# FFN transposes by DMA instead of TensorE, with a new order of work on VectorE and ScalarE

## The chip, the cores and the metric

The kernel runs on one core of a Trainium2 chip. A core has TensorE (PE, with its weight loads PEld), VectorE (DVE), ScalarE (ACT), GpSimd (POOL) and SyncE (SP), which issues DMAs. Each works through its own list of instructions in order; semaphores tie them together. The metric is the time of one execution on the device, in microseconds, lower is better; several runs are summed up by their median.

## The reference

2048 tokens of 512 channels pass through one layer: a linear cross attention, then a gated FFN with quantised weights and activations. The change touches the second part:

```
def activation_quant(x):
    scale = 127.0 / clip(max(abs(x), axis=-1), EPS)
    return clip(round(x * scale), -128, 127) / scale

x   = x + attention(layernorm(x), ctx, ctx, mask, ...)
h   = layernorm(x)
gate = bit_linear(h, w_gate)                # weights -1, 0, 1 times one scale
up   = bit_linear(h, w_up)
a    = up * square(relu(gate))              # 2048 wide
a    = a * rsqrt(mean(square(a)) + 1e-6) * subln_weight
out  = x + bit_linear(a, w_down)            # back to 512 wide
```

`bit_linear` quantises its input by `activation_quant`. So the scale of a row of `a` is known only when all 2048 columns and their squares are there.

## The kernel before

The tokens are 16 tiles of 128 (`NT`). Attention runs first, in four groups of four tiles; beside it the FFN weights are brought to -1, 0, 1 (`tern`, bf16) and the normalised x of groups 0 to 2 is quantised to int8 (`xq`). The last group is quantised within the FFN (`ln2.statistics`, `largest`, `scale`, `quantise`; `cubes` prepares the factors of the scales).

The FFN (`ffn`) is a pipeline over tiles; step s works on tile s with its gate and up products, and on the tiles before it with the rest. For one tile:

- POOL casts `xq` to bf16 `xqb` (L1030, L1033). PE turns it in four 128x128 transposes into PSUM (`turn_x`, L1218), ACT copies it to `xqT` (L1062).
- In four quarters of 512 columns PE computes gate and up (`gate_up`, L1232, 8 products a quarter, two pairs of PSUM banks), ACT takes relu (L1074) and its square, relu2 (L1078), DVE multiplies by up (`multiply`, L1142, writes `acts`), and POOL multiplies by the subln weight (L1048, writes `actg`). ACT sums squares of each half (`squares`, L1085), DVE takes the largest of each half (`largest`, L1147).
- DVE works out the scale in a chain of small operations, `mean` (L1189) to `qs` (L1205), with a square root on ACT (L1108) in it. In the next step it writes the quantised tile `aq` as int16 in one pass (L1156).
- PE turns `aq` in sixteen transposes (L1260) as raw 16-bit patterns, ACT copies them to bf16 `aqT`, changing int16 to bf16 on the way (L1104). A step later PE runs the sixteen down products (L1246), DVE scales them and adds x (`res`, L1167), and SP stores the result (L1016).

The order on each engine is written out by hand. On DVE a step is: multiply 0; aq of the tile before; multiply 1; res of the tile two before; work for the last group of the second layernorm in steps 0 to 7; multiply 2; largest 0; multiply 3; mean, var; largest 1; the rest of the scale. On ACT: quarters 0, 1, 2; copy of xqT; squares 0; quarter 3; squares 1; copies of aqT; square root. On PE: gate_up 0 and 1; down; gate_up 2; turn x; turn aq; gate_up 3. Every engine uses a loop over pairs of steps for the middle of the run. A line `eng.wait_ge(sem, n)` holds the engine until the semaphore has reached n; what follows on that engine waits too.

## Time and profile before

| | us |
|---|---|
| median of 3 runs | 479.37 (477.47 to 481.32) |
| the profiled execution | 475.91 |
| its span from first to last instruction | 474.1 |

The attention takes the first 268 us of the span, the FFN the rest. Busy shares of the page count an engine's instructions; a matmul's end is modelled, so records of PE overlap their successors. "idle before <- releaser" says how long the engine stood before an instruction and what ended that. The page's second part gives the granted clock of PE: full in nearly all of the span, and lower near the end, where PE has little to do.

### The profile page before, as it was taken

Reading aid. Unit: us, or ns where it says so; the run is one execution under the profiler, and the core shown is the slowest. Engines: PE = TensorE matmul, PEld = TensorE weight load, DVE = VectorE, ACT = ScalarE, POOL = GpSimd, SP = SyncE. Lnnn points to the kernel's source line nnn. Section 1 sums busy time; section 2 is a strip of 40 time slices with the busy share of each in tenths; the row PEclk is TensorE's granted clock in tenths of the full one; section 3 lists DMA queues with packets and bytes.
Section 4 is the critical chain, followed back from the end, with each engine's and each line's share of the span. In section 5 each row is a group of like instructions: output and inputs, shape, how many; then the busy total and the mean of one; then the engine's idle time right before and its main releaser. Section 6 shows DMA issues by size and latency. Waiting matters only on the chain. (4 is left out here: it accounts for less than half of the span.)

```text
span 474.1 us, 9209 instructions
## 1 busy us (share of the span) xinstructions
PE 428.0 (90%) x3118; PEld 229.7 (48%) x3136; DVE 382.1 (81%) x869; ACT 338.0 (71%) x538; POOL 155.4 (33%) x145
## 2 busy tenths in 40 slices
PE   4888899997999998999948779999889999999976
PEld 1355546564455653557526334444444444444433
DVE  3588687699989989999898678888888777777772
ACT  5388997494677657775776577777667887888871
POOL 2009200073004600022000145555555555555440
PEclk9998999999899999999987999999999999999999
DMA  7899892004023311232114300000000000000001
GB/s 217 302 395 399 321 365 83 1 2 150 29 91 135 130 47 44 88 99 78 47 45 135 131 1 1 24 22 24 22 25 24 22 24 23 22 22 22 23 24 44
DMA packets 17009, 43.89 MB, mean 93 GB/s; under 512 B 3216, under 2 KB 3216, under 8 KB 16848
## 3 DMA queue, kind: packets, MB, share of 16 engines
q1 hardware_dynamic: 16080, 40.06, 23.7%
q0 software_dynamic: 896, 3.41, 2.0%
q8 instruction: 19, 0.31, 0.3%
q14 instruction: 14, 0.11, 0.1%
HBM read 39.27 MB, written 4.19 MB: 92 GB/s over the span
## 5 line engine op out<-in xcount | busy, mean ns | idle before, releaser
L1048 POOL TENSOR_TENSOR actg<-acts,subln 128x512 f32<-128x512 f32 x64 | 94.7, 1492 | 87.5 <-DVE acts L1142 87.5
L1232 PE MATMUL ps<-tern,xqT 128*128 128x512 bf16 x495 | 113.1, 379 | 4.7 <-DVE acts L1142 1.9
L1232 PEld LDWEIGHTS ps<-tern,xqT 128*128 128x128 bf16 x512 | 48.9, 98 | 61.3 <-DVE acts L1142 4.3
L1246 PE MATMUL ps<-tern,aqT 128*128 128x512 bf16 x255 | 59.2, 385 | 9.5 <-ACT aqT L1104 9.3
L1074 ACT ACTIVATE relu<-ps 128x512 f32<-128x512 f32 x64 | 37.9, 592 | 21.8 <-PE ps L1232 20.9
L1142 DVE TENSOR_TENSOR acts<-relu,ps 128x512 f32<-128x512 f32 x64 | 43.6, 682 | 7.9 <-ACT relu L1078 6.2
L1085 ACT ACTIVATE square<-acts 128x1024 bf16<-128x1024 f32 x32 | 33.7, 1052 | 19.1 <-DVE acts L1142 19.1
L1246 PEld LDWEIGHTS ps<-tern,aqT 128*128 128x128 bf16 x256 | 24.1, 99 | 44.0 <-issue 12.4
L1078 ACT ACTIVATE relu<-relu 128x512 f32<-128x512 f32 x64 | 40.3, 630 | 2.7 <-DVE acts L1142 0.7
L1147 DVE TENSOR_REDUCE amax<-actg 128x1 f32<-128x1024 f32 x32 | 38.8, 1212 | 4.2 <-POOL actg L1048 4.2
L524 DVE SCALAR_TENSOR_TENSOR fl<-ps,fh 128x512 f16<-128x512 f32 x64 | 39.6, 679 | 2.5 <-ACT fh L387 2.5
L387 ACT ACTIVATE qkTh<-ps,bqk 128x512 f16<-128x512 f32 x32 | 21.6, 684 | 21.5 <-PE ps L726 20.6
L387 ACT ACTIVATE fh<-ps 128x512 f16<-128x512 f32 x64 | 33.9, 617 | 2.2 <-PE ps L760 1.7
L343 POOL TENSOR_TENSOR xs<-xs,bob 128x512 f32<-128x512 f32 x16 | 20.8, 1324 | 41.2 <-ACT xno L404 41.2
L387 ACT ACTIVATE xnTh<-ps 128x512 f16<-128x512 f32 x32 | 18.2, 600 | 22.3 <-PE ps L795 22.3
L1104 ACT ACTIVATE aqT<-ps 128x1024 bf16<-128x1024 int16 x32 | 30.7, 1010 | 4.7 <-PE ps L1260 4.7
L440 ACT ACTIVATE wst<-wst,magic,winv_g 128x1024 f32<-128x1024 f32 x24 | 29.9, 1244 | 5.6 <-DMA wst<-in_wffn 5.5
L524 DVE SCALAR_TENSOR_TENSOR qkTl<-ps,bqk,qkTh 128x512 f16<-128x512 f32 x32 | 23.4, 746 | 11.5 <-ACT qkTh L387 11.3
L726 PE MATMUL ps<-ctxh,wkh 128*128 128x512 f16 x64 | 25.3, 395 | 6.9 <-DVE ctxl L513 6.4
L443 ACT ACTIVATE wst<-wst,magic 128x1024 f32<-128x1024 f32 x24 | 27.6, 1149 | 0.8
L726 PE MATMUL ps<-wvh,ctxh 128*128 128x512 f16 x64 | 24.3, 379 | 1.7 <-DVE wvl L517 1.7
L432 ACT ACTIVATE tern<-tern 128x1024 f32<-128x1024 f32 x24 | 25.2, 1056 | 0.0
(166 smaller groups left out, 1012.1 us busy)
## 6 DMA issues: line engine op xcount, KB each, us to landing
tern<-in_wffn SPq DMA_DIRECT2D x24, 512.0 KB, 11.8
wst<-in_wffn SPq DMA_DIRECT2D x24, 512.0 KB, 3.3
xs<-in_x SPq DMA_DIRECT2D x4, 1024.0 KB, 8.0
out<-res SPq DMA_DIRECT2D x16, 256.0 KB, 2.0
ctxf<-in_ctxT POOLq DMA_DIRECT2D x3, 1024.0 KB, 10.8
xno<-in_wkT SPq DMA_DIRECT2D x4, 256.0 KB, 5.4
ctxf<-in_ctxT SPq DMA_DIRECT2D x4, 256.0 KB, 6.1
fh<-in_wvT SPq DMA_DIRECT2D x1, 1024.0 KB, 7.7
```

The costliest lines, as they stand in the source:

```text
L387: nc.scalar.activation(out, in_, func, **kw).then_inc(high[stage], 1)
L524: nc.vector.scalar_tensor_tensor(out=out, in0=in0, scalar=scalar, in1=in1, op0=op0, op1=ALU.subtract).then_inc(drained[stage], 1)
L726: mm = nc.tensor.matmul(acc, a, b, start=first and n == 0, stop=last and n == len(pairs) - 1)
L1048: nc.gpsimd.tensor_tensor(actg[:, s0 % 2, q], acts[:, s0 % 2, q], subln[:, q], ALU.mult)\
L1074: nc.scalar.activation(relu[:, c % 2, :], ps[:, 2 * (c % 2), :], ACT.Relu).then_inc(relu_ok, 1)
L1078: nc.scalar.activation(relu2[:, c % 2, :], relu[:, c % 2, :], ACT.Square).then_inc(relu2_ok, 1)
L1085: nc.scalar.activation(square[:, h], acts[:, s0 % 2, FF // 2 * h:FF // 2 * h + FF // 2], ACT.Square, accum_out=ssq[:, s0 % 2, h:h + 1]).th ...
L1104: nc.scalar.activation(aqT[:, (s0 - 1) % 2, 8 * h:8 * h + 8, :], tbank_i[h], ACT.Copy)\
L1142: nc.vector.tensor_tensor(acts[:, k, 512 * c:512 * c + 512], relu2[:, c % 2, :], ps[:, 2 * (c % 2) + 1, :], ALU.mult).then_inc(acts_ok, 1)
L1147: return nc.vector.tensor_reduce(amax[:, k, h:h + 1], actg[:, k, FF // 2 * h:FF // 2 * h + FF // 2], AX_X, ALU.max, apply_absolute_value=True)
L1232: mm = nc.tensor.matmul(ps[:, 2 * (c % 2) + b, :], xqT[:, s0 % 2, k, :], weights[k][:, 512 * c:512 * c + 512], start=(k == 0), stop=(k == ...
L1246: mm = nc.tensor.matmul(ps[:, 7, :], aqT[:, s0 % 2, k, :], down_w[:, k, :], start=(k == 0), stop=(k == FK - 1))
```

## The change

Both transposes of the FFN become DMA transposes from SBUF to SBUF, issued by SP. For this `aq` must be bf16 with whole numbers in it: ACT multiplies by the scale and adds 1.5 * 2^23, which rounds, and DVE subtracts that again while writing bf16. The PSUM banks that the transposes held go to a third pair for gate and up and a second one for down. `relu2` has four buffers, `xqT` three. Tiles 0 and 1 of x are cast and turned at the end of attention. The order on ACT and DVE is new: the scale of tile s-1 is now worked out in step s. The loops over pairs of steps are written out.

New attention parts, and the FFN's SP queue:

```
            # attention, SP, after the last weight chunks
            for j in range(2):
                sp.wait_ge(xqb_ok, j + 1)
                sp.dma_start_transpose(xqT[:, j], xqb[:, j, :]).then_inc(xqT_in[j], 16)
            # attention, POOL, before its last turn
            pool.wait_ge(winv_ok, 2)
            for j in range(2):
                nc.gpsimd.tensor_copy(xqb[:, j, :], ln2.xq[:, j, :]).then_inc(xqb_ok, 1)
...
            # FFN, SP, after the load of subln
            for s in range(NT + 2):
                j = s + 2
                if j < NT:
                    sp.wait_ge(xqb_ok, j + 1)
                    if j >= XT:
                        sp.wait_ge(U_filled, NB * (j - XT + 1))
                    sp.dma_start_transpose(xqT[:, j % XT], xqb[:, j % 2, :]).then_inc(xqT_in[j % XT], 16)
                if s >= 2:
                    sp.wait_ge(res_ok, s - 1)
                    sp.dma_start(out_dram[s - 2], res[:, s % 2, :]).then_inc(out_done[s % 2], 16)
                if 1 <= s <= NT:
                    sp.wait_ge(aq_ok, s)
                    if s >= 3:
                        sp.wait_ge(D_filled, s - 2)
                    sp.dma_start_transpose(aqT[:, (s - 1) % 2], aq[:, (s - 1) % 2, :])\
                        .then_inc(aqT_in[(s - 1) % 2], 16)
```

ACT and DVE:

```
+            def scaled(s):
+                act.wait_ge(magic_ok, 1)
+                act.wait_ge(qs_ok, s + 1)
+                nc.scalar.activation(actg[:, s % 2, :], actg[:, s % 2, :], ACT.Identity, bias=magic_up[:, :],
+                                     scale=qs[:, s % 2:s % 2 + 1]).then_inc(scaled_ok, 1)
+            for s in range(NT + 1):
+                if s < NT:
+                    quarter(s, 0)
+                if s > 0:
+                    squares(s - 1, 1)
+                if s > 0:
+                    root(s - 1)
+                if s < NT:
+                    quarter(s, 1)
+                if s > 0:
+                    scaled(s - 1)
+                if s < NT:
+                    quarter(s, 2)
+                    squares(s, 0)
+                    quarter(s, 3)
...
+            def quantiser(s):
+                k, col = s % 2, slice(s, s + 1)
+                largest(s, 1)
+                dve.wait_ge(ssq_ok, 2 * s + 2)
+                (mean, var -> var_ok, mx)
+                dve.wait_ge(sd_ok, s + 1)
+                (reciprocal, two steps for nt, cr, my, inv, qs -> qs_ok, dq)
+            def whole(s):
+                dve.wait_ge(scaled_ok, s + 1)
+                if s > 1:
+                    dve.wait_ge(aqT_in[s % 2], landed(s - 2, 2))
+                nc.vector.tensor_scalar(aq[:, s % 2, :], actg[:, s % 2, :], ROUND, None, ALU.subtract)\
+                    .then_inc(aq_ok, 1)
+            for s in range(NT + 2):
+                if s < NT:
+                    multiply(s, 0)
+                if 1 <= s <= NT:
+                    quantiser(s - 1)
+                if s < NT:
+                    multiply(s, 1)
+                    multiply(s, 2)
+                if 1 <= s <= NT:
+                    whole(s - 1)
+                if s < NT:
+                    largest(s, 0)
+                if 1 <= s <= GT:
+                    ln2.statistics(nc, dve, 0, G - 1, s - 1)
...
+                if s >= 2:
+                    result(s - 2)
+                if s < NT:
+                    multiply(s, 3)
```

The three lines in brackets stand for the small operations named, unchanged in kind. Left out above: `ln2.largest` and `ln2.scale` in step 5, `ln2.quantise` in steps 7 and 8, `cubes` in step 9, all ahead of `result`. PE and the host:

```
+            for s in range(NT + 2):
+                if s < NT:
+                    for c in range(NB - 1):
+                        gate_up(s, c)
+                if s >= 2:
+                    down(s - 2)
+                if s < NT:
+                    gate_up(s, NB - 1)
...
-    nc = bacc.Bacc("TRN2", target_bir_lowering=False, num_devices=1)
+    nc = bacc.Bacc("TRN2", target_bir_lowering=False, num_devices=1, dynamic_dma_scratch_size=8192)
```

POOL casts x two tiles ahead, once the turn of the tile that used the buffer has landed, and goes on to multiply by subln quarter by quarter, as before.

## Rows read from the trace of the kernel before

**Rows 1.** The page's first part: busy time, share of the span, instructions, by engine.

```profile
PE 428.0 (90%) x3118; PEld 229.7 (48%) x3136; DVE 382.1 (81%) x869; ACT 338.0 (71%) x538; POOL 155.4 (33%) x145
```

**Rows 2.** Timeline of PE late in the FFN: start us, us, engine, line, what.

```profile
407.90 0.39 PE L1218 MATMUL ps<-identh,xqb 128*128 128x128 bf16 x4
...
409.23 5.13 PE L1232 MATMUL ps<-tern,xqT 128*128 128x512 bf16 x23
...
420.81 5.13 PE L1232 MATMUL ps<-tern,xqT 128*128 128x512 bf16 x23
```

**Rows 3.** Waits in the FFN: who for whom, total us, times, longest.

```profile
ACT relu L1074 <- PE ps L1232: 20.9, 19, 1.4
```

**Rows 4.** Timeline of the FFN's first tile, all engines.

```profile
268.49 0.64 POOL L1033 TENSOR_SCALAR xqb<-xq 128x512 bf16<-128x512 int8 x1 [45.56 <-POOLq L160]
...
270.50 5.13 PE L1232 MATMUL ps<-tern,xqT 128*128 128x512 bf16 x23 [0.92 <-ACT xqT L1062]
...
273.07 0.60 ACT L1074 ACTIVATE relu<-ps 128x512 f32<-128x512 f32 x1 [0.47 <-PE ps L1232]
...
273.70 0.63 ACT L1078 ACTIVATE relu<-relu 128x512 f32<-128x512 f32 x1
274.37 0.69 DVE L1142 TENSOR_TENSOR acts<-relu,ps 128x512 f32<-128x512 f32 x1 [0.98 <-ACT relu L1078]
...
275.13 1.28 POOL L1048 TENSOR_TENSOR actg<-acts,subln 128x512 f32<-128x512 f32 x1 [0.32 <-DVE acts L1142]
...
276.94 0.68 DVE L1142 TENSOR_TENSOR acts<-relu,ps 128x512 f32<-128x512 f32 x1
...
278.76 0.69 DVE L1142 TENSOR_TENSOR acts<-relu,ps 128x512 f32<-128x512 f32 x1
...
280.91 0.21 DVE L1190 TENSOR_SCALAR var<-mean,cube 128x1 f32<-128x1 f32 x1
...
281.16 0.20 ACT L1108 ACTIVATE sdf<-var 128x1 f32<-128x1 f32 x1 [0.53 <-DVE var L1190]
```

**Rows 5.** Timeline late in the FFN: DVE's passes in one step.

```profile
394.98 1.28 DVE L1156 TENSOR_SCALAR aq<-actg,qs 128x2048 int16<-128x2048 f32 x1
...
396.17 0.68 DVE L1142 TENSOR_TENSOR acts<-relu,ps 128x512 f32<-128x512 f32 x1
...
396.77 0.74 DVE L1167 SCALAR_TENSOR_TENSOR res<-ps,dq,xs 128x512 f32<-128x512 f32 x1
...
397.43 0.68 DVE L1142 TENSOR_TENSOR acts<-relu,ps 128x512 f32<-128x512 f32 x1
...
398.67 1.22 DVE L1147 TENSOR_REDUCE amax<-actg 128x1 f32<-128x1024 f32 x1 [0.56 <-POOL actg L1048]
...
399.80 0.68 DVE L1142 TENSOR_TENSOR acts<-relu,ps 128x512 f32<-128x512 f32 x1
```

**Rows 6.** Timeline of the last tile: down, and the chain of the scale.

```profile
460.51 4.99 PE L1246 MATMUL ps<-tern,aqT 128*128 128x512 bf16 x16 [3.39 <-ACT aqT L1104]
...
461.17 0.20 ACT L1108 ACTIVATE sdf<-var 128x1 f32<-128x1 f32 x1
...
461.40 0.17 DVE L1195 RECIPROCAL rstdf<-sdf 128x1 f32<-128x1 f32 x1
...
462.81 0.21 DVE L1205 TENSOR_SCALAR qs<-inv,cr 128x1 f32<-128x1 f32 x1
```

**Rows 7.** Groups of ACT by line: busy us, mean ns, idle before.

```profile
L440 ACT ACTIVATE wst<-wst,magic,winv_g 128x1024 f32<-128x1024 f32 x24 | 29.9, 1244 | 5.6 <-DMA wst<-in_wffn 5.5
L404 ACT ACTIVATE xno<-xs,shift,rstd 128x512 f32<-128x512 f32 (+1 forms) x16 | 12.1, 810 | 0.5 <-DVE shift L545 0.5
```

**Rows 8.** The page's DMA issues: count, KB each, median us to landing.

```profile
tern<-in_wffn SPq DMA_DIRECT2D x24, 512.0 KB, 11.8
wst<-in_wffn SPq DMA_DIRECT2D x24, 512.0 KB, 3.3
...
out<-res SPq DMA_DIRECT2D x16, 256.0 KB, 2.0
```

More of the change, by code:

```diff
@@ L300, in _ @@
             chunks(0, G - 1, CPM - 2)
+            for j in range(2):
+                sp.wait_ge(xqb_ok, j + 1)
+                sp.dma_start_transpose(xqT[:, j], xqb[:, j, :]).then_inc(xqT_in[j], 16)
         @block.gpsimd
@@ new lines, in quarter @@
+            def quarter(s, c):
+                u = NB * s + c
+                act.wait_ge(G_filled, u + 1)
+                if u >= 2:
+                    act.wait_ge(relu2_ok, u - 1)
+                nc.scalar.activation(relu[:, u % 2, :], gate_bank(u), ACT.Relu).then_inc(relu_ok, 1)
+                act.wait_ge(relu_ok, u + 1)
+                if u >= R2:
+                    act.wait_ge(acts_ok, u - R2 + 1)
+                nc.scalar.activation(relu2[:, u % R2, :], relu[:, u % 2, :], ACT.Square).then_inc(relu2_ok, 1)
@@ new lines, in squares, with root @@
+            def squares(s, h):
+                act.wait_ge(acts_ok, NB * s + 2 * h + 2)
+                if s > 0:
+                    act.wait_ge(ssq_ok, 2 * s + h - 1)
+                nc.scalar.activation(square[:, h], acts[:, s % 2, HALF * h:HALF * h + HALF],
+                                     ACT.Square, accum_out=ssq[:, s % 2, h:h + 1]).then_inc(ssq_ok, 1)
+            def root(s):
+                act.wait_ge(var_ok, s + 1)
+                nc.scalar.activation(sd[:, :], var[:, :], ACT.Sqrt).then_inc(sd_ok, 1)
@@ L1117, in _ @@
             link = Chain(dve, chain)
+            link.start()
             def cubes(c):
@@ new lines, in multiply, with largest @@
+            def multiply(s, c):
+                u = NB * s + c
+                dve.wait_ge(relu2_ok, u + 1)
+                dve.wait_ge(U_filled, u + 1)
+                nc.vector.tensor_tensor(acts[:, s % 2, 512 * c:512 * c + 512], relu2[:, u % R2, :],
+                                        up_bank(u), ALU.mult).then_inc(acts_ok, 1)
+            def largest(s, h):
+                dve.wait_ge(actg_ok, NB * s + 2 * h + 2)
+                return nc.vector.tensor_reduce(amax[:, s % 2, h:h + 1],
+                                               actg[:, s % 2, HALF * h:HALF * h + HALF], AX_X,
+                                               ALU.max, apply_absolute_value=True)
@@ L1207, in _, with result @@
-            steps(dve, step, link, 9)
+            def whole(s):
+                dve.wait_ge(scaled_ok, s + 1)
+                if s > 1:
+                    dve.wait_ge(aqT_in[s % 2], landed(s - 2, 2))
+                nc.vector.tensor_scalar(aq[:, s % 2, :], actg[:, s % 2, :], ROUND, None, ALU.subtract)\
+                    .then_inc(aq_ok, 1)
+            def result(s):
+                dve.wait_ge(D_filled, s + 1)
+                if s > 1:
+                    dve.wait_ge(out_done[s % 2], landed(s - 2, 2))
+                nc.vector.scalar_tensor_tensor(out=res[:, s % 2, :], in0=down_bank(s), scalar=dq[:, s % 2:s % 2 + 1],
+                                               in1=xs[:, s, :], op0=ALU.mult, op1=ALU.add).then_inc(res_ok, 1)
@@ new lines, in _ @@
+            for s in range(NT + 2):
[12 more added lines that the diff above has]
+                    ln2.statistics(nc, dve, 0, G - 1, s - 1)
+                if s == GT + 1:
+                    ln2.largest(nc, dve, link)
+                if s == SCALE2_AT:
+                    ln2.scale(nc, dve, link, 0, G - 1)
+                if s in QUANTISE2_AT:
+                    half = 2 * QUANTISE2_AT.index(s)
+                    ln2.quantise(nc, link, 0, G - 1, (half, half + 1))
+                if s == CUBES2_AT:
+                    cubes(slice(NT - GT, NT))
+                if s >= 2:
+                    result(s - 2)
+                if s < NT:
+                    multiply(s, 3)
@@ L1268, in _, with gate_up @@
-            steps(pe, step)
+            def gate_up(s, c):
+                u = NB * s + c
+                pe.wait_ge(xqT_in[s % XT], landed(s, XT))
+                for weights, acc, free, fill in ((gate_w, gate_bank(u), relu_ok, G_filled),
+                                                 (up_w, up_bank(u), acts_ok, U_filled)):
+                    if u >= PAIRED:
+                        pe.wait_ge(free, u - PAIRED + 1)
+                    for k in range(KC):
+                        mm = nc.tensor.matmul(acc, xqT[:, s % XT, k, :], weights[k][:, 512 * c:512 * c + 512],
+                                              start=(k == 0), stop=(k == KC - 1))
+                    mm.then_inc(fill, 1)
@@ new lines, in down @@
+            def down(s):
+                pe.wait_ge(aqT_in[s % 2], landed(s, 2))
+                if s >= 2:
+                    pe.wait_ge(res_ok, s - 1)
+                for k in range(FK):
+                    mm = nc.tensor.matmul(down_bank(s), aqT[:, s % 2, k, :], down_w[:, k, :],
+                                          start=(k == 0), stop=(k == FK - 1))
+                mm.then_inc(D_filled, 1)
+            for s in range(NT + 2):
+                if s < NT:
+                    for c in range(NB - 1):
+                        gate_up(s, c)
+                if s >= 2:
+                    down(s - 2)
+                if s < NT:
+                    gate_up(s, NB - 1)
```

279 lines of the change are left out of this document (54 added, 225 removed).

## The prediction

> **What bounds the kernel now.** I read the page first, for which engines are full. TensorE and VectorE are both near four fifths or more of the span, ScalarE follows, GpSimd is far from full [rows 1]. That is a mean over attention and FFN, so the next view is the timeline of the FFN late in the run, where tiles repeat. One tile takes 420.81 - 409.23 = 11.58 us. TensorE's own work explains all of it: 48 products of 512 columns at 5.13/24 = 0.214 us (the row counts 23 records of 24) are 10.26 us, and from the first transpose of x to the first product behind the transposes 409.23 - 407.90 = 1.33 us pass, so 11.59 [rows 2]. In the steady part TensorE is the bound. The waits agree: ScalarE's largest wait in the FFN is for TensorE's gate product, 20.9 us in all [rows 3].
>
> **What the change removes.** Both kinds of transposes leave TensorE, 1.33 us a tile. With nothing else in the way a tile would come down to 10.26 us. ScalarE loses the two passes that copy turned tiles out of PSUM. The first FFN product no longer waits for the first turned x: the FFN begins at 268.5 and the first product at 270.50 [rows 4], so up to 2.0 us are saved once, because tiles 0 and 1 are turned during attention. The casts for that are two of 0.6 us on GpSimd, which had been idle for 45.56 us when the FFN began [rows 4], and their two transfers stand behind the last weight chunk on SP's queue, some 8 us ahead of their use. Cost nothing; if that cover is gone, one transfer's length, once. The smaller scratch for GpSimd's transfers and the dropped identh touch only early work: nothing, with an upper bound of a microsecond or two.
>
> **What it adds, and where the path goes.** The transfers are one matter, the new order of three in-order engines another, and the second decides. I follow one tile round, from the last multiplication of a step, `multiply(s-1, 3)`, to the last of the next step, `multiply(s, 3)`. In the new order every link is either a semaphore or the order on one engine:
>
> 1. multiply (VectorE) to actg (GpSimd): 275.13 - 274.37 = 0.76; actg 1.28 and 0.05 to VectorE, 1.33 [rows 4].
> 2. `quantiser(s-1)` begins with `largest(s-1, 1)`, which waits for that actg: 1.13 (399.80 - 398.67) [rows 5]. In the kernel before, the square root ran beneath this reduction; now the reduction stands ahead of it.
> 3. mean, a linked small operation, 0.24; var to the square root on ScalarE 281.16 - 280.91 = 0.25 [rows 4]; square root to the reciprocal 0.23, reciprocal to qs 462.81 - 461.40 = 1.41 [rows 6]; qs to ScalarE as var to ScalarE, 0.25.
> 4. `scaled(s-1)`, new, 2048 columns. No row has it. The nearest have the same kind of operands: 0.81 us for 512 columns, 1.24 for 1024 [rows 7]. 0.43 for each further 512 gives 2.10. Bounds: 1.9 and 2.4.
> 5. ScalarE only then comes to `quarter(s, 2)`: relu 0.63 (273.70 - 273.07), relu2 0.67 until the multiplication may start (274.37 - 273.70) [rows 4].
> 6. VectorE: `multiply(s, 2)` 0.60 (396.77 - 396.17; a result takes 397.43 - 396.77 = 0.66), then `whole(s-1)` behind it, taken like the pass that wrote aq, 396.17 - 394.98 = 1.19, `largest(s, 0)` 1.13, `result(s-2)` 0.66, and `multiply(s, 3)` [rows 5].
>
> Sum: 0.76 + 1.33 + 1.13 + 0.24 + 0.25 + 0.23 + 1.41 + 0.25 + 2.10 + 0.63 + 0.67 + 0.60 + 1.19 + 1.13 + 0.66 = 12.6 us. No tile can be quicker than this ring however early TensorE delivers: 1.0 us above the 11.58 of now. A third pair of banks and four relu2 buffers don't open it, since none of its links is a wait for a free bank. Added up singly, the new work of ScalarE and of VectorE is only about 9 us a tile each. Neither is full; each waits for the other.
>
> All that VectorE does between `largest(s, 0)` and `result` lies in the ring too. Statistics in four steps: 276.94 - 274.37 - 0.60 = 1.97 each [rows 4], 7.9. The largest, scale and cubes: about 24 linked small operations at 0.22, taken from the chain of six in 1.41 us [rows 6], 5.3. Quantising four tiles: four passes of 512 columns at 0.60, 2.4. Together 15.6 us, which in the kernel before lay partly beneath TensorE.
>
> **The transfers.** The aq tile is 512 KB and its turning is shown by no row. The nearest are a plain load of 512 KB in 3.3 us on a lightly used queue and in 11.8 us on a full one [rows 8]. In the FFN the queue is light, so the value lies near the lower end; I take 5 for the crossing of rows and columns. It matters through SP's queue: there the turn of aq(s-1) is queued behind the store of `result(s-2)`, which waits for `down(s-2)`. Second ring: down 16 x 0.214 = 3.4, result and handovers 0.9, issue of the store 0.3, transfer L, so 4.6 + L. It overtakes the 12.6 at L = 8. Below that the transfer is hidden, except once at the end; each microsecond above 8 costs some 15 us. x is a quarter of the size, is asked for more than a step ahead, and costs nothing.
>
> A rule bears on L. The Trainium skill (Advanced Engine Details and Errata, X-Bar Transpose) says that transposing transfers are as fast as ordinary ones; by it L would be the 3.3 of the plain load and the whole result 2 us lower. Against the change speaks the Trainium skill (VectorE: DVE Perf Modes, The three transpose paths): 1.309 us for one 128x128 block by DMA. Sixteen in series would be an estimated 21 us and a tile of 25.6 us, about 700 us for the kernel. No row of this trace decides between them.
>
> **The sum.** Mark of tile 0, `multiply(0, 3)`: 278.76 now [rows 4], less 2.0, 276.8. Fifteen rounds of 12.58 are 188.7. VectorE's extras 15.6, less one result that step 1 doesn't have, 0.7: mark of tile 15 at 480.4. Tail: links 1 to 4, 7.7; whole 1.28; result(14) 0.74; handovers and issue 0.3 (490.4); transfer 5 (495.4); down: 3.4 at the upper clock, but after 3.39 idle us the last-but-one down of now took 4.99 [rows 6], and here the pause is longer, so 5.0 (500.4); result 0.74; store 2.0 and its issue 0.3: 503.4. The span of now is 474.1, so +29.3 us. The profiled execution took 475.9 and the median of the runs is 479.4; the difference is put on the median: 508.7, say 509.
>
> **Rivals.**
> - *The transfer is the bound.* A turn of 512 KB moves in pieces that a plain load doesn't have. For: nothing in the kernel before measures it, and the loaded case took 11.8 us [rows 8]. Against: the queue is nearly empty here. At L = 11.8 a tile takes 4.6 + 11.8 = 16.4; fifteen of them from the first down at about 297 are 543, with the last down, result and store 553, so some 558 against the median. It decides from L = 8. Chance 0.17, over all L above 8. The block rate above, as a mechanism, is in it with 0.04.
> - *TensorE's floor is reached; the kernel gets faster.* Three bank pairs and an x turned two tiles ahead let TensorE run ahead, and VectorE's and ScalarE's 9 us a tile fit beneath 10.26. Mark of tile 0 at 276.8, fifteen tiles of 10.3 are 154, tail 23: 454, and 459 against the median. For it: the busy sums. Against it: it needs a way out of the ring, whose links leave none; it breaks even where the ring is 29.3/15 = 2.0 us shorter, 10.6. Chance 0.07.
> - *The gain and the ring cancel.* The handovers are shorter than I read them and the extras find a gap, so a tile takes about 11: 480 to 490. Chance 0.06.
>
> **How the numbers follow.** Forecast (ring of three engines) 0.70, its own range 498 to 520: `scaled` between 1.9 and 2.4 moves it by -3 to +5, L from 3.3 to 8 by -2 to +10, pauses that lower the clock by 0 to +5. For 8 in 10 the range takes in the lower edge of the cancelling case and L up to 10: 495 to 535. Faster by over 1% 0.08, within 1% 0.04 (about what a measurement here can tell from no change), slower 0.88.
>
> **What would show it.** Right: marks of `multiply(s, 3)` some 12.5 us apart late in the FFN; TensorE idle 2 us a tile before down or a gate product; VectorE's waits for ScalarE's relu2 and for GpSimd's actg ahead of `largest(s, 1)`, ScalarE's for var and qs. `scaled` near 2.1, whole near 1.28, the turn of aq 3.3 to 8 us from issue to landing. Wrong: tiles of 10.3 to 11 us; `scaled` well under 2; downs that wait for a transfer of more than 8 us.

## The result, and the profile after

The changed kernel takes 505.02 us, median of 4 runs (503.24 to 508.13), against 478.42 for the kernel before beside it: ratio 1.0553, interval 1.048 to 1.0626. It is slower. Its profiled execution has a span of 503.0 us.

The page of the kernel after, first two parts (busy time by engine; granted clock in 40 slices):

```profile
PE 427.7 (85%) x2816; PEld 215.7 (43%) x2816; DVE 376.7 (75%) x869; ACT 334.1 (66%) x506; POOL 154.8 (31%) x145
...
PEclk9999999998999999999789987998988999989878
```

Against [rows 1] every engine's share has fallen. TensorE has 302 matmul records fewer and the same 428 us, because part of its work now runs at the lower clock: its down products take 73.8 us in place of 59.2, and most of the digits of 7 and 8 lie in the FFN (from slice 22), where the kernel before has 9s. No engine bounds this kernel by its own work, so the next view is one step, on all engines. Timeline of the kernel after, late in the FFN (start us, us, engine, line, what, idle before and its releaser):

```profile
427.11 0.68 DVE L1116 TENSOR_TENSOR acts<-relu,ps 128x512 f32<-128x512 f32 x1
...
427.87 1.28 POOL L1038 TENSOR_TENSOR actg<-acts,subln 128x512 f32<-128x512 f32 x1 [1.32 <-DVE acts L1116]
...
429.18 1.22 DVE L1121 TENSOR_REDUCE amax<-actg 128x1 f32<-128x1024 f32 x1 [0.28 <-POOL actg L1038]
...
430.32 0.20 DVE L1130 TENSOR_SCALAR mean<-ssq 128x1 f32<-128x1 f32 x1
...
430.81 0.20 ACT L1065 ACTIVATE sdf<-var 128x1 f32<-128x1 f32 x1 [1.59 <-DVE var L1131]
...
431.04 0.17 DVE L1135 RECIPROCAL rstdf<-sdf 128x1 f32<-128x1 f32 x1
...
432.38 0.21 DVE L1143 TENSOR_SCALAR qs<-inv,cr 128x1 f32<-128x1 f32 x1
...
432.70 2.09 ACT L1071 ACTIVATE actg<-actg,magic_up,qs 128x2048 f32<-128x2048 f32 x1 [0.54 <-DVE qs L1143]
...
432.78 3.63 PE L1212 MATMUL ps<-tern,aqT 128*128 128x512 bf16 x16 [1.58 <-DMA aqT<-aq]
...
434.70 0.57 ACT L1049 ACTIVATE relu<-ps 128x512 f32<-128x512 f32 x1
435.30 0.63 ACT L1053 ACTIVATE relu<-relu 128x512 f32<-128x512 f32 x1
...
435.96 0.69 DVE L1116 TENSOR_TENSOR acts<-relu,ps 128x512 f32<-128x512 f32 x1 [2.70 <-ACT relu L1053]
...
436.57 1.22 DVE L1152 TENSOR_SCALAR aq<-actg 128x2048 bf16<-128x2048 f32 x1
436.73 2.19 POOL L1038 TENSOR_TENSOR actg<-acts,subln 128x512 f32<-128x512 f32 x1 [2.12 <-DVE acts L1116]
...
437.70 1.21 DVE L1121 TENSOR_REDUCE amax<-actg 128x1 f32<-128x1024 f32 x1
...
438.83 0.74 DVE L1160 SCALAR_TENSOR_TENSOR res<-ps,dq,xs 128x512 f32<-128x512 f32 x1
...
439.49 0.68 DVE L1116 TENSOR_TENSOR acts<-relu,ps 128x512 f32<-128x512 f32 x1
```

From `multiply(s-1, 3)` at 427.11 to `multiply(s, 3)` at 439.49 are 12.38 us, where the kernel before had 11.58 a tile [rows 2]. Read it with a finger on the chain: multiply, GpSimd's product, reduction, scale, square root, scale, the 2048-column pass, relu, relu2, multiply, `aq`, reduction, result, multiply. Each entry begins when the one ahead lets it, on three engines in turn. VectorE stands 2.70 us for relu2, which stands behind the 2.09 us pass on ScalarE, which waits for `qs`.

The waits of the kernel after within the FFN (who for whom: total us, times, longest), with the times to landing from the issues of its DMAs:

```profile
DVE acts L1116 <- ACT relu L1053: 48.2, 25, 2.7
PE ps L1212 <- DMA aqT<-aq: 37.9, 13, 5.7
ACT sdf L1065 <- DVE var L1131: 27.1, 16, 1.8
ACT relu L1049 <- PE ps L1202: 20.1, 21, 3.7
DVE amax L1121 <- POOL actg L1038: 10.7, 14, 1.4
```

```profile
xqT<-xqb SPq DMA_TRANSPOSE x16, 2.9
aqT<-aq SPq DMA_TRANSPOSE x16, 4.4
```

ScalarE's wait for TensorE, 20.1 us, is about the 20.9 of [rows 3], but VectorE's wait for ScalarE has grown from 6.2 to 48.2. The line that looks like the culprit is the second: TensorE waits 37.9 us for the turned `aq`. It isn't yet shown to cost anything: the timeline has `down` beginning at 432.78 while ScalarE is in its long pass, and the step's length is explained without it. That is the question of the experiments.

### The profile page after: what moved, and what is told of

The parts are those of the page before. It is cut to its first block and busy times, and to the rows that moved or that the text cites. A ratio compares the mean times of both kernels' runs of the same rounds, so it can differ in the third digit from the quotient of the medians.

```text
span 503.0 us, 8338 instructions
## 1 busy us (share of the span) xinstructions
PE 427.7 (85%) x2816; PEld 215.7 (43%) x2816; DVE 376.7 (75%) x869; ACT 334.1 (66%) x506; POOL 154.8 (31%) x145
## 5 line engine op out<-in xcount | busy, mean ns | idle before, releaser
L1202 PE MATMUL ps<-tern,xqT 128*128 128x512 bf16 x512 | 114.6, 380 | 8.2 <-DVE acts L1116 6.1
L1212 PE MATMUL ps<-tern,aqT 128*128 128x512 bf16 x256 | 73.8, 454 | 38.0 <-DMA aqT<-aq 37.9
L1116 DVE TENSOR_TENSOR acts<-relu,ps 128x512 f32<-128x512 f32 x64 | 43.1, 683 | 48.2 <-ACT relu L1053 48.2
L1212 PEld LDWEIGHTS ps<-tern,aqT 128*128 128x128 bf16 x256 | 27.8, 113 | 84.1 <-DMA aqT<-aq 45.3
L1049 ACT ACTIVATE relu<-ps 128x512 f32<-128x512 f32 x64 | 37.3, 583 | 20.1 <-PE ps L1202 20.1
L1060 ACT ACTIVATE square<-acts 128x1024 bf16<-128x1024 f32 x32 | 33.5, 1046 | 15.6 <-DVE acts L1116 15.5
L1071 ACT ACTIVATE actg<-actg,magic_up,qs 128x2048 f32<-128x2048 f32 x16 | 33.5, 2094 | 9.8 <-DVE qs L1143 9.8
L536 DVE SCALAR_TENSOR_TENSOR qkTl<-ps,bqk,qkTh 128x512 f16<-128x512 f32 x32 | 23.4, 747 | 11.5 <-ACT qkTh L399 11.3
L738 PE MATMUL ps<-ctxl,wkh 128*128 128x512 f16 x64 | 25.7, 402 | 0.0
L738 PE MATMUL ps<-ctxh,wkl 128*128 128x512 f16 x64 | 25.5, 399 | 0.0
```

Source lines behind the costliest of these rows:

```text
L536: nc.vector.scalar_tensor_tensor(out=out, in0=in0, scalar=scalar, in1=in1, op0=op0, op1=ALU.subtract).then_inc(drained[stage], 1)
L738: mm = nc.tensor.matmul(acc, a, b, start=first and n == 0, stop=last and n == len(pairs) - 1)
L1049: nc.scalar.activation(relu[:, u % 2, :], gate_bank(u), ACT.Relu).then_inc(relu_ok, 1)
L1060: nc.scalar.activation(square[:, h], acts[:, s % 2, HALF * h:HALF * h + HALF], ACT.Square, accum_out=ssq[:, s % 2, h:h + 1]).then_inc(ssq_ ...
L1071: nc.scalar.activation(actg[:, s % 2, :], actg[:, s % 2, :], ACT.Identity, bias=magic_up[:, :], scale=qs[:, s % 2:s % 2 + 1]).then_inc(sca ...
L1116: nc.vector.tensor_tensor(acts[:, s % 2, 512 * c:512 * c + 512], relu2[:, u % R2, :], up_bank(u), ALU.mult).then_inc(acts_ok, 1)
```

## The experiments

The kernels of one group ran on one chip, beside runs of the kernel before: 476.8 us for the first group, 476.7 for the second, 477.6 for the third. "Late tiles" is the distance between the starts of VectorE's pass that writes `aq`, near the end of the FFN, where the second layernorm's work is over and the clock is not lowered. Where the late tiles of a run differ, it is the shortest that comes more than once, and the text says so. A "round" goes from `multiply(s-1, 3)` to `multiply(s, 3)`.

### First group: which ring, and what is in it

**half_scaled** halves one link of the ring on ScalarE.

```
-                nc.scalar.activation(actg[:, s % 2, :], actg[:, s % 2, :], ACT.Identity, ...
+                nc.scalar.activation(actg[:, s % 2, 0:HALF], actg[:, s % 2, 0:HALF], ACT.Identity, ...
```

> The kernel after, with ScalarE's pass `scaled` over the first 1024 of the 2048 columns only; VectorE still subtracts over all of them, so the other half of the tile is left unscaled and unrounded, and nothing else is left out. Theory (ring of VectorE, GpSimd and ScalarE): `scaled` falls from 2.09 to about 1.2 us and stands in the ring, so a late tile goes from 12.4 to 11.5 us and the kernel loses 15 x 0.88 plus 0.9 in the tail, 14 us: 491. Rival (each tile waits for the turn of aq, 4.4 us from issue to landing): the turn is as long as before, no more than 1 us is gained, 504. Rival (ScalarE or TensorE is simply full): ScalarE's share falls but the time by at most 2 us.

Measured: 493.28 us, ratio 1.0323 (1.0251 to 1.0395). The pass takes 1.24 us in place of 2.09, and late tiles take 11.52 in place of 12.38 at their shortest (the last six rounds are 11.82 on the mean, against 12.62). So 0.85 us of work on an engine that is busy 66% of the span took up to 0.86 off a tile. Over the whole run about 11 us came back, under the 14 expected. The fifteen rounds are 9.8 us shorter, not 15 x 0.86 = 12.9: some ran at the lower clock, and in others (11.78 and 11.81 us at the upper one) down stood for the transfer, 1.98 us in one of them, and ScalarE's last relu behind it. With the ring shorter, the transfer begins to show.

**half_turn** halves the transfer that TensorE waits for.

```
-                    sp.dma_start_transpose(aqT[:, (s - 1) % 2], aq[:, (s - 1) % 2, :])\
+                    sp.dma_start_transpose(aqT[:, (s - 1) % 2, 0:FK // 2], aq[:, (s - 1) % 2, 0:HALF])\
...
-                    mm = nc.tensor.matmul(down_bank(s), aqT[:, s % 2, k, :], down_w[:, k, :],
+                    mm = nc.tensor.matmul(down_bank(s), aqT[:, s % 2, k % 8, :], down_w[:, k, :],
```

> The kernel after, with only the first 1024 columns of aq turned, and each half of the down products using the same eight turned blocks: sixteen products as before, half the transfer; the second half of the down input is left out. Theory (ring): the transfer, some 3 us instead of 4.4, lies beside the ring; only the last one shows, 1 to 2 us, and fewer long pauses of TensorE may give back 1 to 2 more: 502 to 504, late tiles 12.4. Rival (the transfer bounds a tile): each of fifteen tiles is 1.4 us shorter, 484.

Measured: 500.24 us, 1.0501 (1.0436 to 1.0566), an interval that overlaps that of the changed kernel; the median is 1.8 us below what was expected. The turn lands after 3.1 us in place of 4.4, and late tiles still take 12.38. So in this order the 37.9 us of waiting for the transfer are nearly all free: the longest-looking wait of TensorE is not the cause.

**double_turn** puts two half turns into a spare buffer ahead of the real one.

```
+                    for h in range(2):
+                        sp.dma_start_transpose(aqT2[:, h], aq[:, (s - 1) % 2, HALF * h:HALF * h + HALF])\
+                            .then_inc(aqT_in[(s - 1) % 2], 16)
                     sp.dma_start_transpose(aqT[:, (s - 1) % 2], aq[:, (s - 1) % 2, :])\
```

> The kernel after, with the same aq turned a second time, in two halves, into a spare buffer ahead of the turn that is used; down waits for all three. Issue to landing of the whole goes from 4.4 to 6.6 if the fixed part is shared, to 8.8 if not. Theory (ring 12.4, second ring of transfer, down, result and store 4.6 + L): up to L = 8 it costs 2 to 4 us at the end and some pauses, 507 to 512; at 8.8 the second ring is 13.4 and costs some 15 to 20: 520 to 525. Rival (the transfer bounds a tile already): the full 2.2 to 4.4 us in each of 15 tiles, 538 to 571.

Measured: 529.64 us, 1.1105 (1.1042 to 1.1168). That is 4.6 us above the upper of the two ranges expected, and that range was for a transfer of 8.8 us, where 8.05 came. Timeline of double_turn, one round between two downs:

```profile
447.69 5.31 PE L1216 MATMUL ps<-tern,aqT 128*128 128x512 bf16 x16 [3.35 <-DMA aqT<-aq]
...
453.04 0.75 DVE L1164 SCALAR_TENSOR_TENSOR res<-ps,dq,xs 128x512 f32<-128x512 f32 x1 [1.35 <-PE ps L1216]
453.82 0.34 SPq L1014 DMA_DIRECT2D out<-res  x1
...
454.26 2.65 SPq L1020 DMA_TRANSPOSE aqT<-aq  x2
...
462.31 3.63 PE L1216 MATMUL ps<-tern,aqT 128*128 128x512 bf16 x16 [2.40 <-DMA aqT<-aq]
```

This is the prediction's second ring: down, result, store, turn, down. The turns take 8.05 us from the first issue to the next down (454.26 to 462.31). `aq` of that tile was ready at 450.6, and its turn stood behind the store on SP all the same. The round is 14.6 us long, of which 1.7 is this down's lower clock (5.31 against 3.63). Without that it would be 12.9, so at 8 us of transfer this ring is already a little longer than the first one. Its parts other than the transfer are 4.9 us by these rows, where the prediction had 4.6, so it overtakes 12.38 at some 7.5 us of transfer, which is an estimate from this one round. The late steps vary between 12.37 and 16.25 us, and eight of the fifteen rounds ran in part at the lower clock, so the price of each microsecond beyond that is not shown.

**scaled_after_q2** moves the long pass behind `quarter(s, 2)` on ScalarE, so that relu and relu2 of that quarter no longer stand behind it.

```
                     quarter(s, 1)
+                if s < NT:
+                    quarter(s, 2)
                 if s > 0:
                     scaled(s - 1)
                 if s < NT:
-                    quarter(s, 2)
                     squares(s, 0)
```

> The kernel after with two entries of ScalarE's order exchanged: `quarter(s, 2)` ahead of `scaled(s-1)`. Nothing is left out. Theory (ring): relu and relu2 of quarter 2 no longer stand behind `scaled`, and run while VectorE is at the chain of the scale; the ring becomes 0.76 + 1.33 + 1.13 + 0.24 + 0.25 + 0.11 + 2 x 1.18 + 2.15 + 1.19 + 1.13 + 0.66 = 11.3 us, 1.1 less than the 12.4 measured, about 17 us over the kernel: 488. Rival (a transfer or a full engine is the bound): no work has gone, so the time stays within 2 us of 505.

Measured: 493.59 us, 1.0334 (1.0256 to 1.0413): about 5 us over what was expected. Late tiles take 11.52 at their shortest, not 11.3, and the last six rounds are 11.92 on the mean. Timeline of scaled_after_q2:

```profile
412.26 2.51 POOL L1038 TENSOR_TENSOR actg<-acts,subln 128x512 f32<-128x512 f32 x2 [2.42 <-DVE acts L1117]
...
413.12 3.63 PE L1213 MATMUL ps<-tern,aqT 128*128 128x512 bf16 x16 [3.30 <-DMA aqT<-aq]
...
414.24 1.62 DVE L1153 TENSOR_SCALAR aq<-actg 128x2048 bf16<-128x2048 f32 x1 [1.30 <-ACT actg L1071]
...
417.64 0.60 ACT L1049 ACTIVATE relu<-ps 128x512 f32<-128x512 f32 x1 [2.40 <-PE ps L1203]
```

The pass that writes `aq` takes 1.62 us in place of 1.22. GpSimd's two products end at 414.77, and 414.77 + 1.09 is the end of the pass: it stood until GpSimd was done. In the changed kernel it is the other way round: `aq` starts first (436.57, done at 437.79), and GpSimd's product beside it takes 2.19 in place of 1.28 (436.73 to 438.92, that is 1.13 after the end of `aq`). The Trainium skill (SBUF — State Buffer, Who interferes with whom) has this: VectorE, in its two-port modes, and GpSimd share one pair of ports, which goes whole to whichever instruction is issued first. Both directions agree with it here, 0.4 us the one way and 0.9 the other.

The other two rows show what else was missed. This round is 12.89 us long at the upper clock. The turn of `aq` stood behind the store on SP, down stands 3.30 us for it, and relu of the last quarter stands 2.40 us for the gate product behind down. A transfer that is hidden beside a ring of 12.4 us is no longer hidden beside one of 11.5.

### Second group: what the parts are worth, and a way out

**old_order** keeps the DMA transposes and the pass on ScalarE, but has the order of VectorE and ScalarE as before: the scale of tile s is worked out at the end of step s, `aq` follows behind `multiply(s+1, 0)`.

```
-            for s in range(NT + 1):
-                if s < NT:
-                    quarter(s, 0)
...
+            for s in range(NT):
+                quarter(s, 0)
+                quarter(s, 1)
...
+                quarter(s, 2)
+                squares(s, 0)
+                quarter(s, 3)
+                squares(s, 1)
+                root(s)
+                scaled(s)
```

> The kernel after with the transposes by DMA and the pass `scaled` kept, but the order on VectorE and ScalarE taken back to that of the kernel before: the scale of tile s at the end of step s, `scaled(s)` as ScalarE's last work of the step, `whole(s-1)` after the next step's first multiplication, the result after its second. Nothing is left out. Theory (the order of three in-order engines sets the time): here the ring runs from the end of one step to the next through the whole of `scaled` and the relu behind it, with nothing of ScalarE beneath it, 13.6 us a late tile, so the new order is worth something, but not enough: 516 to 522 against 505 for the kernel after. Rival (the new order is what costs, the DMA transposes gain): without it the kernel is at or below the kernel before, 465 to 479.

Measured: 523.7 us, 1.0967 (1.0913 to 1.1021), 1.7 us above what was expected, late tiles 13.87. So the new order is no loss in itself: with the extra pass given, it takes 1.5 us a tile off. In old_order the pass waits 42.3 us in all for `qs`, with the next tile's first relu behind it on ScalarE, and TensorE waits for that relu.

**dve_round** takes the pass off ScalarE altogether: VectorE scales and rounds to int16 in one pass and turns that into bf16 in a second.

```
-                nc.vector.tensor_scalar(aq[:, s % 2, :], actg[:, s % 2, :], ROUND, None, ALU.subtract)\
-                    .then_inc(aq_ok, 1)
+                dve.wait_ge(qs_ok, s + 1)
+                link(nc.vector.tensor_scalar(aqi[:, :], actg[:, s % 2, :], qs[:, s % 2:s % 2 + 1], None, ALU.mult))
+                nc.vector.tensor_copy(aq[:, s % 2, :], aqi[:, :]).then_inc(aq_ok, 1)
```

> The kernel after without `scaled` on ScalarE: VectorE multiplies by the scale into int16, which rounds, as the kernel before did, and then copies int16 to bf16, which DMA turns. Order and everything else as in the kernel after, nothing left out. Theory (ring): `scaled` and its two handovers leave the ring, which becomes VectorE's own work with GpSimd's last pass, 0.76 + 1.33 + 1.13 + 0.24 + 0.25 + 0.23 + 1.41 + 1.2 + 1.19 + 1.13 + 0.66 = 9.5 and the copy of 2048 columns, 0.35 to 1.2, so 9.9 to 10.7; with pauses for transfers 10.5 to 11.2 a late tile and 470 to 482 for the kernel. Rival (VectorE or a transfer is the bound): VectorE gets more work, so it is slower than 505.

Measured: 499.14 us, 1.0461 (1.0413 to 1.0509), late tiles 11.96. That is a miss, by 17 us and more. Timeline of dve_round:

```profile
417.87 3.49 POOL L1039 TENSOR_TENSOR actg<-acts,subln 128x512 f32<-128x512 f32 x2 [2.41 <-DVE acts L1115]
418.46 1.77 DVE L1151 TENSOR_SCALAR aqi<-actg,qs 128x2048 int16<-128x2048 f32 x1
...
420.26 1.64 DVE L1152 CAST aq<-aqi 128x2048 bf16<-128x2048 int16 x1
```

GpSimd's first product ends at 417.87 + 1.28 = 419.15, and the int16 pass at 420.23, 1.08 later: it lost half a microsecond standing. Then GpSimd's second product goes first, ends at 421.36, and the cast ends 0.54 us later, at 421.90. It takes 1.64 us; in the last tile, with no product beside it, it takes 0.69. Two fast passes on VectorE meet two passes on GpSimd, and the four go one after the other. The expectation had added durations measured with nothing beside them: the two delays together are 1.4 us a tile. No run takes them out, so that they are the whole miss is read from the trace and not shown.

**warm** adds six products of 512 columns on TensorE ahead of each down, in a stretch in which it would stand.

```
+                for k in range(6):
+                    nc.tensor.matmul(down_bank(s), xqT[:, min(s + 2, NT - 1) % XT, 0, :], down_w[:, k, :],
+                                     start=True, stop=True)
+                pe.wait_ge(aqT_in[s % 2], landed(s, 2))
```

> The kernel after with six products of 512 columns, whose result is overwritten, ahead of TensorE's wait for the turned aq in each tile; nothing is left out. They take 1.3 us of a pause of 1.6 to 2.3. Theory: the late steps of 13.8 us between steps of 12.4 are those where the granted clock fell to its lower level after a pause; with the pause filled they go, and the time is 500 to 504; the other steps stay at 12.4, since TensorE isn't in the ring. Rival (TensorE's work counts): 1.3 us more in each tile, 520 or more.

Measured: 503.68 us, 1.0581 (1.0521 to 1.0641). The granted clock over the FFN rises from 0.91 to 0.96, all late steps take 12.37 or 12.38, and the time is the same within the intervals. So the digits of 7 and 8 on the page are an effect of TensorE's pauses. They cost little: in the two profiled executions the fifteen rounds take 198.9 us with the products and 200.8 without them.

**deep** opens the ring: the scale of tile s-1 is worked out in step s as before, but the long pass, `aq` and the turn follow only in step s+1, and down another step later.

```
+            for s in range(NT + 2):
+                if 1 <= s <= NT:
+                    squares(s - 1, 0)
+                if s >= 2:
+                    scaled(s - 2)
                 if s < NT:
                     quarter(s, 0)
...
-                if s >= 2:
-                    down(s - 2)
+                if s >= 3:
+                    down(s - 3)
```

VectorE's order is then: both `largest` of s-1, multiply 0, `whole(s-2)`, multiply 1, `variance(s-1)`, multiply 2, `result(s-3)`, `scale(s-1)`, multiply 3. `root(s-1)` stands ahead of `quarter(s, 3)` on ScalarE. SP issues the turn of x, the turn of `aq`, then the store.

> The kernel after with its steps spread over one more: the scale of tile s-1 is worked out in two parts in step s (both reductions ahead of the first multiplication, the variance after the second, the scale after the third), `scaled(s-2)`, `whole(s-2)` and the turn follow in the step after that, and down, result and store handle tile s-3. Banks and buffers as they are, nothing left out. Theory: the ring is spread over two steps, so it no longer holds a tile; TensorE's 10.26 us become the bound, and the transfer has more than half a step: late tiles 10.3 to 10.6, a tail one down longer, 452 to 462 for the kernel, quicker than both. Rival (the transfer or a full engine holds a tile at 11.5 or more): 475 or more.

Measured: 468.73 us, 0.9817 (0.977 to 0.9865), late tiles 10.49. It is quicker than the kernel before, but 7 us short of the expected range. Timeline of deep:

```profile
408.34 3.74 POOL L1039 TENSOR_TENSOR actg<-acts,subln 128x512 f32<-128x512 f32 x3 [2.69 <-DVE aq L1157]
...
409.23 0.21 DVE L1131 TENSOR_SCALAR mean<-ssq 128x1 f32<-128x1 f32 x1
...
411.04 1.06 DVE L1138 TENSOR_TENSOR mx<-amax 128x1 f32<-128x1 f32 x1
```

`mx` is one element a partition and takes 1.06 us. GpSimd's three products end at 412.08, `mx` ends at 412.10. `mean`, with one tensor in SBUF for input, ran beside the same products in 0.21. `mx` has two. One caution on the cause of the gain: deep also moves both reductions ahead of the first multiplication and changes ScalarE's order, and no run separates that from the tile more in flight.

### Third group: the turn alone, and the small operations

**turn_alone** has the DMA transposes without the pass on ScalarE: `aq` stays int16, written in one pass on VectorE as before, the DMA turns the 16-bit patterns into `aqTi`, and ScalarE copies that to bf16. The order of VectorE and ScalarE is that of before.

```
-        aq = sb("aq", [P, 2, FF], BF16)
+        aq = sb("aq", [P, 2, FF], I16)
         aqT = sb("aqT", [P, 2, FK, P], BF16)
+        aqTi = sb("aqTi", [P, 2, FK, P], I16)
...
+            def turned(s):
+
+                act.wait_ge(aqT_in[s % 2], landed(s, 2))
+                if s > 1:
+                    act.wait_ge(D_filled, s - 1)
+                for h in range(2):
+                    nc.scalar.activation(aqT[:, s % 2, 8 * h:8 * h + 8, :], aqTi[:, s % 2, 8 * h:8 * h + 8, :],
+                                         ACT.Copy).then_inc(aqT_ok, 1)
```

> The transposes by DMA alone: order, int16 tile and ScalarE's copies to bf16 as in the kernel before (x still turned two tiles ahead, three pairs of banks as in the kernel after), the int16 tile turned by DMA into a spare buffer and copied from there. Nothing is left out. TensorE loses its 1.33 us a tile, ScalarE only the copy of x. Theory (VectorE and ScalarE, in their order, stand close behind TensorE): in the old order VectorE waits for the square root, which stands behind ScalarE's squares and copies; laid out with the durations of the rows that round is 11.5 us, hardly below the 11.6 of now, so the DMA transposes by themselves are worth nothing that can be told from no change: 472 to 482 against 477. Rival (TensorE is the only bound, and DMA transposes gain when nothing else is changed): 16 x 1.33 less, 456 to 460. Rival (DMA transposes themselves cost): 490 or more.

Measured: 485.47 us, 1.0177 (1.0138 to 1.0216), late tiles 11.82: 3.5 us above what was expected. Timeline of turn_alone, and below it two rows of the kernel before, late in the FFN:

```profile
416.30 1.99 ACT L1074 ACTIVATE aqT<-aqTi 128x1024 bf16<-128x1024 int16 x2
...
418.34 3.63 PE L1215 MATMUL ps<-tern,aqT 128*128 128x512 bf16 x16 [1.29 <-ACT aqT L1074]
...
421.80 4.48 PE L1205 MATMUL ps<-tern,xqT 128*128 128x512 bf16 x20
...
422.86 0.60 ACT L1050 ACTIVATE relu<-ps 128x512 f32<-128x512 f32 x1 [2.20 <-PE ps L1205]
```

```profile
413.23 1.92 ACT L1104 ACTIVATE aqT<-ps 128x1024 bf16<-128x1024 int16 x2
...
414.29 3.63 PE L1246 MATMUL ps<-tern,aqT 128*128 128x512 bf16 x16
```

The transposes have left TensorE, and it stands 1.29 us ahead of down for the copies instead, with the next gate product, and ScalarE's relu, behind that down. But one thing is not as it was. In the kernel before, down waits for each half of the copied tile by itself: the copies run from 413.23 to 415.15, and down starts at 414.29, 0.06 us after the first of the two. Here it waits for both, and starts 2.04 us after the copies begin in place of 1.06. That 0.98 us lies in the chain (relu, multiply, squares, copies, down, gate product, relu), so of the 11.82 us some 10.84 would be left without it. This is an estimate, and no run shows it. It would put the DMA transposes alone, in the old order, 0.7 us a tile below the kernel before. So turn_alone does not show that the removal alone brings nothing. It shows that a second chain, through ScalarE's copies, lies between TensorE's products and the old 11.58, and takes away a part of the gain.

**deep_one_input** is deep with four small operations (`mx`, `nt`, `cr`, `dq`) of the scale written so that each has one tensor input, the other value coming in as a scalar of the partition.

```
-                nc.vector.tensor_tensor(mx[:, :], amax[:, k, 0:1], amax[:, k, 1:2], ALU.max)
+                nc.vector.tensor_scalar(mx[:, :], amax[:, k, 0:1], amax[:, k, 1:2], None, ALU.max)
...
-                link(nc.vector.scalar_tensor_tensor(out=nt[:, :], in0=rstd[:, :], scalar=rstd[:, 0:1],
-                                                    in1=var[:, :], op0=ALU.mult, op1=ALU.mult))
+                link(nc.vector.tensor_scalar(nt[:, :], rstd[:, :], rstd[:, 0:1], var[:, 0:1], ALU.mult, ALU.mult))
```

> The kernel of the run deep, in which four small operations of VectorE on 128x1 (mx, nt, cr, dq) are written as tensor_scalar with the second operand as a per-partition scalar instead of as a second input tensor. Same work, nothing left out. Theory (a VectorE operation with two input tensors in SBUF waits for the end of the GpSimd pass under way; one with a single input tensor doesn't): mx goes from a mean of 0.70 to 0.15 and nt from 0.78 to 0.22, VectorE, which is full in the first ten steps, gets 1.1 us a step back there, the late steps stay at 10.5 where TensorE is the bound: 8 to 10 us less, 459 to 463. Rival (those two are long because of what went before them on VectorE): mx and nt stay long and the time at 468.

Measured: 454.04 us, 0.9537 (0.9495 to 0.9579), below the expected range. All sixteen instances of `mx` and of `nt`, in deep and then in deep_one_input (ns: min/median/max, first and last start):

```profile
L1138 DVE TENSOR_TENSOR mx<-amax x16: 151/466/1121, 282.8 to 450.4; 128x1 f32<-128x1 f32 x16
L1141 DVE SCALAR_TENSOR_TENSOR nt<-rstdf,var x16: 218/1118/1126, 283.8 to 450.7; 128x1 f32<-128x1 f32 x16
```

```profile
L1138 DVE TENSOR_SCALAR mx<-amax x16: 202/203/208, 282.0 to 435.2; 128x1 f32<-128x1 f32 x16
L1141 DVE TENSOR_SCALAR nt<-rstdf,var x16: 272/273/276, 282.3 to 435.5; 128x1 f32<-128x1 f32 x16
```

Written with one input they cost 50 ns more at their best, and always that. The same section of the Trainium skill names instructions with two SBUF inputs as contending with a GpSimd instruction that reads SBUF; these rows agree. TensorE of deep_one_input, the starts of two downs:

```profile
402.98 3.62 PE L1219 MATMUL ps<-tern,aqT 128*128 128x512 bf16 x16
...
413.34 3.62 PE L1219 MATMUL ps<-tern,aqT 128*128 128x512 bf16 x16
```

10.36 us a tile: that is 48 products 0.216 us apart with nothing between them, so TensorE is the bound here. (The 10.26 worked out from [rows 2] is 0.1 too low.) Measured on VectorE the same tiles are 9.74 apart. VectorE is catching up there with a lag built up earlier: from the last gate or up product of a tile to its last multiplication it is 4.38 us in tile 10 and 1.17 in tile 15. Where that lag came from was not examined.

### The steps together

| kernel | late tiles, us | ratio | the turn | extra pass | order |
|---|---|---|---|---|---|
| before | 11.58 | 1 | TensorE | none | old |
| turn_alone | 11.82 | 1.0177 | DMA | none | old, down waits for both copies |
| old_order | 13.87 | 1.0967 | DMA | ScalarE | old |
| after | 12.38 | 1.0553 | DMA | ScalarE | new |
| scaled_after_q2 | 11.52 (mean 11.92) | 1.0334 | DMA | ScalarE | new, one exchange |
| dve_round | 11.96 | 1.0461 | DMA | VectorE | new |
| deep | 10.49 | 0.9817 | DMA | ScalarE | one step deeper |
| deep_one_input | 9.74 (TensorE 10.36) | 0.9537 | DMA | ScalarE | one step deeper |

## Why the prediction was right

It had the sign, the cause and the size: 509 us and a range of 495 to 535 were given, 505.0 came. In spans it was 503.4 forecast and 503.0 measured; the rest of the difference is the 5.3 us that it put on for the step from the span to the median, where 2.1 were needed. Point by point:

- **The ring.** 12.58 us forecast, 12.38 measured. The largest new term, the 2048-column pass on ScalarE, was interpolated at 2.10 from [rows 7] and took 2.09. The 0.2 us too much are in small links: the next relu starts 2.00 us after the pass does (2.10), reciprocal to `qs` is 1.34 (forecast 1.41), relu and relu2 to the multiplication 1.26 (1.30), the pass writing `aq` 1.13 from start to start (1.19); `qs` to ScalarE is 0.32 (0.25), the other way. Over fifteen rounds 3.0 us.
- **That a ring bounds, and which.** half_scaled and scaled_after_q2 show it by shortening it (up to 0.86 us a tile each), half_turn by changing nothing when the transfer is shorter, and deep by opening it: 10.49 us a tile with the same passes, the same transfers and one tile more in flight.
- **VectorE's extras.** Forecast 15.6 less 0.7. Measured, the rounds from the first mark at 277.28 to the last at 478.07 are 200.8, less 15 x 12.38 = 185.7 leaves 15.1, and 1.4 of that is in two late rounds (13.57 and 12.63), in the first of which down ran at the lower clock. So the extras themselves are at most 13.7; in warm, where the clock hardly falls, the same sum is 13.2. Three of the four rounds with statistics are 14.32 long, 1.94 over the others (forecast 1.97), and the fourth, without a result, 13.65. The small operations and the quantising were put 1.1 to 1.6 us too high. (`ln2.scale` stands in step 6, not in step 5 as the list ahead of the rows has it.)
- **The transfer.** 5 us forecast, 4.4 measured, and hidden except at the end. By the rule of the Trainium skill (Advanced Engine Details and Errata, X-Bar Transpose) that transposing transfers are as fast as ordinary ones it would have been 3.3; by the block rate of the Trainium skill (VectorE: DVE Perf Modes, The three transpose paths) 21. The first is near, the second is far off for this size: 256 KB took 3.1 us (half_turn) and 512 KB 4.4. The ring through SP's queue exists, as double_turn showed, and is the longer one at 8.05 us of transfer.
- **The ends.** The first mark came 1.5 us earlier than before, not 2.0. The turned x was there, but GpSimd stood 4.3 us until the subln weights had landed, and VectorE's first reduction stood 0.96 us for GpSimd, a wait that the prediction hadn't put into the start. The tail was 24.9 us, not 23.0: the last but one down ran at the lower clock, 5.73 us, and ended after `aq` did, so that it held up the result and the last turn.
- **The sum.** Here errors cancel. Start +0.5, rounds 200.8 - 203.6 = -2.8, tail +1.9: together -0.4, and 503.0 came where 503.4 was forecast. That agreement is better than its parts.

Timeline of the kernel before, its last `multiply(15, 3)`, and of the kernel after, its first `multiply(0, 3)` (the row holds `multiply(1, 0)` too), its last, and its last two downs:

```profile
457.58 0.69 DVE L1142 TENSOR_TENSOR acts<-relu,ps 128x512 f32<-128x512 f32 x1 [0.36 <-ACT relu L1078]
```

```profile
277.28 1.36 DVE L1116 TENSOR_TENSOR acts<-relu,ps 128x512 f32<-128x512 f32 x2
...
478.07 0.68 DVE L1116 TENSOR_TENSOR acts<-relu,ps 128x512 f32<-128x512 f32 x1
...
483.07 5.73 PE L1212 MATMUL ps<-tern,aqT 128*128 128x512 bf16 x16 [5.56 <-DMA aqT<-aq]
...
494.49 5.14 PE L1212 MATMUL ps<-tern,aqT 128*128 128x512 bf16 x16 [5.69 <-DMA aqT<-aq]
```

So the 28.9 us by which the span grew are -1.5 at the start, 200.8 - 178.8 = 22.0 in the rounds, and 24.9 - 16.5 = 8.4 in the tail, where the scale, the long pass, `aq` and the transfer stand end to end.

**What the prediction did not see.** It treated VectorE and GpSimd as independent. In this order that was harmless: GpSimd's product beside `aq` is late by 0.9 us, and has time to spare. But it tells in the experiments: in scaled_after_q2, in dve_round, and most clearly between deep and deep_one_input.

It also read TensorE's own work of the kernel before a little wrongly. Timeline of its weight loads:

```profile
408.96 4.90 PEld L1232 LDWEIGHTS ps<-tern,xqT 128*128 128x128 bf16 x24
```

There are 24 loads where [rows 2] has 23 products. The products recorded start 0.216 us apart from 409.23, so the missing first one began at about 409.02. The transposes then take 1.12 us and not 1.33, and the 48 products 10.36 and not 10.26. The sum is 11.48, and the last 0.1 us of the tile is TensorE standing for the first copy of `aqT`, as the two rows beside turn_alone show. So TensorE was the bound, but a chain through ScalarE was level with it. "With nothing else in the way" a tile would come down to 10.26, the prediction says; by turn_alone something was in the way, at 10.8 by the estimate there.

## What to carry to other kernels

When an order over several in-order engines is rewritten, add up the longest closed round through it before anything else: an engine at 66% busy can set the pace, and the largest wait in the list (here 37.9 us for a transfer) may cost nothing. A faster part shortens such a ring (0.86 us here), until the next one shows; one more tile in flight, with the order that goes with it, took off 1.9. Small operations of VectorE beside a busy GpSimd are best written with one tensor input and the rest as scalars of the partition. An experiment that puts an old order back must also put back its waits: one wait for both halves in place of two changed the answer of turn_alone.

## What the runs showed of the hardware

- A DMA transpose between SBUF buffers lands 4.4 us after its issue for 512 KB of bf16 (4.3 to 5.5), 3.1 for 256 KB (half_turn), 2.9 for 128 KB (2.4 to 4.9), each a median. Its issue held SP's queue in the changed kernel for 1.6 to 3.3 us (512 KB) or 1.2 to 2.1 (128 KB), where a plain store took 0.33.
- A VectorE operation on one element a partition took up to 1.12 us in place of 0.15 or 0.22 when it had two inputs in SBUF and GpSimd was at work (deep). With one input it took 0.20 to 0.28 at all times (deep_one_input). The reduction over 1024 columns took 1.21 us beside GpSimd and alone.
- A 2048-column VectorE pass (f32 to bf16 or int16) and a GpSimd product exclude each other, whichever starts first: 1.22 became 1.62 (scaled_after_q2), and 1.28 became 2.19 (the changed kernel). An int16-to-bf16 cast of 2048 columns took 1.64 beside a product and 0.69 without one (dve_round).
- After a pause ahead of a down, TensorE's granted clock fell to the lower level (1.2 GHz) in part of the FFN: 0.91 on the mean against 0.99 in the kernel before. The downs that it caught took 5.1 to 6.2 us in place of 3.6. With six spare products ahead of each down the mean was 0.96 and the time the same.
